# Four graph layers on one core: norm transfers first, gate and both attention layers in column groups, the sort in three pieces, the projection behind the dense loop

## The reference

```python
x = layernorm(x + gate(x, src, dst))
# g = tanh(x[dst] @ w_dst + x[src] @ w_src + b); z[dst] += x[src] * g * 0.5 * norm[dst] * norm[src]
x = layernorm(x + gat(gat(x)))
# per layer, two heads: h = x @ W; logits = leaky_relu(a_s.h[src] + a_d.h[dst], 0.2), self edges added
# a = softmax of the logits over the edges of one dst; out[dst] += h[src] * a
x = layernorm(x + cos(x, src, dst))
# softmax over each dst of beta * cosine(x[dst], x[src]); out[dst] += alpha * x[src]
x = layernorm(x + ((x + segsum(relu(x[src] + edge_attr @ Wl + bl), dst)) @ Wn + bn))
```

## Time and profile before

| what | us |
| --- | --- |
| median of 3 runs | 4987.31 (4984.94 to 4987.55) |
| the profiled execution's own time | 4982.04 |
| its span | 4980.2 |
| busy: PE / DVE / ACT / POOL | 1413.6 / 2485.9 / 960.6 / 3104.6 |
| setup and norms | 0 to 82.45 |
| node block | 82.45 to 1326.5 |
| gate block | 1326.5 to 1537.3 |
| attention 1 / attention 2 | to 2224.0 / to 2916.7 |
| cosine / message | to 3983.9 / to 4980.2 |

### The profile page before, as it was taken

The page is one execution under the profiler, slowest core; times in us unless marked ns, Lnnn a source line. Parts: engine busy times, 40 slices in busy tenths (PEclk is TensorE's granted clock), DMA queues, the critical chain, the costliest instruction groups (busy, mean ns, idle before and its releaser), DMA issues. The chain is left out here.

```text
span 4980.2 us, 34974 instructions
## 1 busy us (share of the span) xinstructions
PE 1413.6 (28%) x5413; PEld 1227.2 (25%) x5413; DVE 2485.9 (50%) x5048; ACT 960.6 (19%) x2420; POOL 3104.6 (62%) x2417
## 2 busy tenths in 40 slices
PE   2887047772031000763400000000000075053121
PEld 2887046762031000542200000000000054042111
DVE  4665036661387819763058853335664343252354
ACT  1554024441021000221100012221000044032010
POOL 6777777777405761017761037777648777787687
PEclk9555555555555555555555555555555576556555
DMA  3665135552011110223402345553001155243011
GB/s 79 183 187 164 21 87 137 138 141 49 3 40 36 22 21 2 80 80 90 113 19 59 104 112 144 144 144 102 15 11 18 19 157 138 66 113 91 16 18 17
DMA packets 285614, 395.98 MB, mean 80 GB/s; under 512 B 125970, under 2 KB 130829, under 8 KB 285562
## 3 DMA queue, kind: packets, MB, share of 16 engines
q1 hardware_dynamic: 170362, 322.94, 21.8%
q0 software_dynamic: 115200, 72.57, 8.9%
HBM read 183.71 MB, written 210.76 MB: 79 GB/s over the span
## 5 line engine op out<-in xcount | busy, mean ns | idle before, releaser
L754 PE MATMUL banks<-ident,cross_in 125*2 125x125 f32 (+3 forms) x26 | 10.5, 405 | 2210.7 <-DVE cross_in L777 1559.2
L210 POOL DMA_INDIRECT edge_rows<-x_rows,src_i x400 | 489.4, 1224 | 151.4 <-issue 151.4
L540 PE MATMUL banks<-node_w,x_t 65*125 65x200 f32 x1600 | 550.4, 535 | 0.0
L754 PEld LDWEIGHTS banks<-ident,cross_in 125*2 125x2 f32 (+3 forms) x26 | 3.0, 117 | 2215.3 <-DVE cross_in L777 1562.3
L540 PEld LDWEIGHTS banks<-node_w,x_t 65*125 65x125 f32 x1600 | 513.0, 328 | 4.7 <-issue 0.3
L210 POOL DMA_INDIRECT edge_rows<-h_rows,src_i x200 | 242.6, 1213 | 409.2 <-POOLq L1318 333.7
L210 POOL DMA_INDIRECT edge_rows<-x_rows,key_i x200 | 250.1, 1250 | 366.5 <-DMA norm_s<-sorted_pairs 296.7
L223 POOL DMA_INDIRECT x_rows<-r_x,src_scat_i x200 | 258.6, 1293 | 120.4 <-issue 60.6
L210 POOL DMA_INDIRECT edge_rows<-x_rows,dst_place_i x200 | 272.3, 1362 | 74.1 <-issue 74.1
L210 POOL DMA_INDIRECT edge_rows<-in_x_dram,src_i x200 | 254.6, 1273 | 78.1 <-issue 71.7
L223 POOL DMA_INDIRECT norm_rows<-edge_rows,scat_i x200 | 256.5, 1282 | 75.0 <-issue 75.0
(11 more groups left out here) (321 smaller groups left out, 4824.9 us busy)
## 6 DMA issues: line engine op xcount, KB each, us to landing
h_rows<-r_h SPq DMA_DIRECT2D x125, 462.0 KB
x_rows<-r_x SPq DMA_DIRECT2D x125, 241.5 KB
x_rows<-r_x SPq DMA_DIRECT2D x125, 224.0 KB
r_x<-x_rows SPq DMA_DIRECT2D x125, 224.0 KB
x_rows<-n_out SPq DMA_DIRECT2D x125, 224.0 KB
n_in<-in_x_dram SPq DMA_DIRECT2D x100, 224.0 KB
n_c<-x_rows SPq DMA_DIRECT2D x100, 224.0 KB
out_dram<-n_out SPq DMA_DIRECT2D x100, 224.0 KB
```

Source lines behind the costliest of these rows:

```text
L210: g.indirect_dma_start(out=to[:, j, :] if len(to.shape) == 3 else to[:, j:j + 1], out_offset=None, in_=table, in_offset=bass.IndirectOffse ...
L540: done = pe.matmul(product[h][:, n // 2, n % 2, :], x_t[u][:, at:at + P], node_w[:, :], start=True, stop=True)
L754: pe.transpose(bank[0][0:cols, 0:rows], frm, ident[0:rows, 0:rows]).then_inc(s_tout, 1)
```

## The change

PALL is 125, as P is, and where planes and rows "over all partitions" are named anew they are the same tiles. The constants, blocks and waits change as follows.

- **Node block**: POOL's transfers are put in the order norm scatters, norm gathers, x[src], x[dst]; the dots leave the node loop. The gate block is merged into it: behind the loop DVE sorts (piece one of three: 36 exchanges and 8 direct steps, and 30 and 54 exchanges in the pieces that follow; before, piece one had 91 and piece two 29), does the x[src] dots, and then the gate group by group of 32, 40, 40, 40, 32 and 16 columns, each behind the arrival of its x[dst] columns. A group's scans start from the last column of the group before. PE, ACT and SP have the projection between the node loop and the gate, in a form that starts the transposition of the next chunk before the product of this one.
- **First segments**: no carry is added to all columns any more. What comes from the partition before only changes the row at the end of the partition's first segment, and is put right at the block's end: one row per partition is fetched (`first_i`), corrected and scattered back.
- **Attention 1 and 2**: no maximum over the segment ahead of the exponents. A running maximum and a running sum are kept per head; the scans of the features are scaled at each column by the change of the maximum. After each group's scans, the node's own edge is merged, ACT makes the own rows (sixteen activations of 125x64 per chunk) and DVE adds them. POOL weighs nothing any more. In attention 2, PE adds the five terms of a chunk by matmuls with the identity and nothing is centred, as the weights are centred in the setup.
- **Scans**: a link stands behind every second scan, everywhere.
- **Cosine and message blocks**: the groups of columns are the new ones; the last has two chunks.

```diff
-GROUPS = (0, 10, 18, 22, 24, 25)
+PALL = 125
+GROUPS = (0, 4, 9, 14, 19, 23, 25)
+SCANS_BETWEEN = 2
...
 def sum_rows_dve(dve, rows, carry):
     for f in range(D):
         done = dve.tensor_tensor_scan(rows[:, :, f], cont[:, :], rows[:, :, f], 0.0, ALU.mult, ALU.add)
-    v.link(done)
+        if f % SCANS_BETWEEN == SCANS_BETWEEN - 1:
+            v.link(done)
...
-CUT = STEPS.index(("direct", SLOT_BITS - 1))
-PARTS = ((0, CUT), (CUT, len(STEPS)))
+CUTS = [0, STEPS.index(("direct", F_BITS + 1)), STEPS.index(("direct", F_BITS + 4)), len(STEPS)]
+PARTS = list(zip(CUTS, CUTS[1:]))
...
-gather(g, xs, x, src_i, s_gx, range(START[1], J))
-gather(g, xd, x, dst_i, s_gx)
-scatter(g, NORM, norm_place, scat_i, J, s_sn)
-g.wait_ge(s_sn, ALL)
-gather(g, norm_place_src, NORM, src_i, s_gn)
+scatter(g, NORM, norm_place_all, scat_i_all, J, s_norms)
+g.wait_ge(s_norms, 16 * J)
+gather(g, norm_place_src_all, NORM, src_i_all, s_norms)
+gather(g, xs_all, x, src_i_all, s_gx, range(START[1], J))
+gather_groups(g, xd_all, x, dst_i_all)
+for u in range(U):
+    g.wait_ge(s0.stored[u], ROWS_DONE * ((ECH + 1 - u) // 2))
+g.indirect_dma_start(out=fetched, out_offset=None, in_=X1,
+                     in_offset=bass.IndirectOffsetOnAxis(ap=first_i[:, :], axis=0)).then_inc(s_first, 16)
+g.wait_ge(s0.row, ECH + 1)
+g.indirect_dma_start(out=X1, out_offset=bass.IndirectOffsetOnAxis(ap=first_scat_i[:, :], axis=0), in_=first_x1, in_offset=None,
+                     bounds_check=last_row(g, ROWS), oob_is_err=False).then_inc(s_first, 16)
...
-nodes_dve(dve, gate_dots)
+nodes_dve(dve)
+sort_fill_dve(dve)
...
+sort_dve(dve, PARTS[0], held[0], held[1])
...
-sum_rows_dve(dve, xs, carry_rows[0])
+for n, (start, end) in enumerate(groups):
+    a, b = start * NC, end * NC
+    c = slice(a, b)
+    dve.wait_ge(s_got[n], got_done(n, 1))
+    dots(xd, 0, heads[0], (start, end))
+    dve.tensor_tensor(heads[0][:, c], heads[0][:, c], heads[1][:, c], ALU.add).then_inc(s0.tanh_in, 1)
+    dve.wait_ge(s0.tanh, n + 1)
+    v.link(dve.scalar_tensor_tensor(heads[0][:, c], heads[0][:, c], 0.5, norm_d[:, c], ALU.mult, ALU.mult))
+    v.link(dve.tensor_tensor(heads[0][:, c], heads[0][:, c], norm_place_src[:, c, 0], ALU.mult))
+    for i in range(start, end):
+        w = slice(i * NC, i * NC + NC)
+        v.link(dve.tensor_tensor(xs[:, w, :], xs[:, w, :], wide(heads[0][:, w]), ALU.mult))
+    for f in range(D):
+        done = dve.tensor_tensor_scan(xs[:, c, f], cont[:, c], xs[:, c, f], xs[:, a - 1, f:f + 1] if a else 0.0, ALU.mult, ALU.add)
+        if f % SCANS_BETWEEN == SCANS_BETWEEN - 1:
+            v.link(done)
+    for i in range(start, end):
+        step(i)
...
-dve.wait_ge(s_shared, 1)
-sums = (xa[:, :, 0:D], vb)
-for h in range(H):
-    sum_rows_dve(dve, sums[h], carry_rows[h])
+def running_softmax(dve, s, rows, at, n, sums, weigh):
+    a, b = (NC * c for c in groups[n])
+    c = slice(a, b)
+    for h in range(H):
+        done = dve.tensor_tensor(scales[:, 2 + h, c], rows[:, c, at + h], dens[h][:, c], ALU.add)
+    v.link(done)
+    for h in range(H):
+        done = dve.scalar_tensor_tensor(scales[:, 2 + h, c], scales[:, 2 + h, c], 0.2, scales[:, 2 + h, c], ALU.mult, ALU.max)
+    v.link(done)
+    for h in range(H):
+        done = dve.tensor_tensor_scan(peaks[:, h, a + 1:b + 1], pen_f[:, c], scales[:, 2 + h, c], peaks[:, h, a:a + 1], ALU.add, ALU.max)
+    v.link(done)
+    for h in range(H):
+        dve.tensor_tensor(scales[:, 2 + h, c], scales[:, 2 + h, c], peaks[:, h, a + 1:b + 1], ALU.subtract)
+        done = dve.tensor_tensor(scales[:, h, c], peaks[:, h, a:b], peaks[:, h, a + 1:b + 1], ALU.subtract)
+    v.link(done)
+    for h in range(H):
+        done = dve.scalar_tensor_tensor(scales[:, h, c], scales[:, h, c], 0.0, pen_f[:, c], ALU.min, ALU.add)
+    done.then_inc(s.args, 1)
+    dve.wait_ge(s.exps, 2 * n + 1)
+    for h in range(H):
+        done = dve.tensor_tensor_scan(masses[:, h, c], scales[:, h, c], scales[:, 2 + h, c], masses[:, h, a - 1:a] if a else 0.0, ALU.mult, ALU.add)
+    v.link(done)
+    for i in range(*groups[n]):
+        v.link(weigh(dve, slice(i * NC, i * NC + NC)))
+    for h in range(H):
+        for f in range(D):
+            done = dve.tensor_tensor_scan(sums[h][:, c, f], scales[:, h, c], sums[h][:, c, f], sums[h][:, a - 1, f:f + 1] if a else 0.0, ALU.mult, ALU.add)
+            if f % SCANS_BETWEEN == SCANS_BETWEEN - 1:
+                v.link(done)
...
+for n, (start, end) in enumerate(groups):
+    dve.wait_ge(s_got[n], got_done(n, 2))
+    running_softmax(dve, s1, xa, D + 1, n, sums, weigh)
+    merge_own(dve, s1, n, 1.0)
+    for i in range(start, end):
+        u, c, w = i % 2, slice(i * NC, i * NC + NC), slice((i - start) * NC, (i - start) * NC + NC)
+        parts = (n_sq[u], n_in[u])
+        for h in range(H):
+            done = dve.tensor_tensor(parts[h][:, :, :], sums[h][:, c, :], wide(mixes[:, h, w]), ALU.mult)
+        v.link(done)
+        dve.wait_ge(s1.own, i + 1)
+        for h in range(H):
+            done = dve.tensor_tensor(e_dup[u][:, :, h, :], e_dup[u][:, :, h, :], parts[h][:, :, :], ALU.add)
+        done.then_inc(s1.x, 1)
...
+def own_chunk(i):
+    u = i % 2
+    act.wait_ge(s1.loaded[u], ROWS_DONE * (i // 2 + 1))
+    if i >= 2:
+        act.wait_ge(s1.turned, i - 1)
+        act.wait_ge(s1.mixed[u], ROWS_DONE * (i // 2))
+    for c in range(NC):
+        at = i * NC + c
+        for h in range(H):
+            done = nc.scalar.activation(e_dup[u][:, c, h, :], r_x1[u][:, c, 0:D], ACT.Copy, scale=tops[h][:, at:at + 1])
+    done.then_inc(s1.own, 1)
...
-project_pe(pe)
...
-project_act(act)
...
-project_sp(sp)
+project_pe(pe)
+project_act(act)
+project_sp(sp)
...
+    terms = (n_in[u][:, :, :], n_c[u][:, :, :], r_x1[u][:, :, 0:D], e_dup[u][:, :, 0, :], e_dup[u][:, :, 1, :])
+    for k, term in enumerate(terms):
+        done = pe.matmul(cols3(bank[1 + i % 4][0:P, :]), ident[0:P, 0:P], term, start=k == 0, stop=k == len(terms) - 1)
+    done.then_inc(s2.y, 1)
```

1100 lines of the change are left out of this document (684 added, 416 removed).

## The result

The changed kernel takes 4604.09 us (median of 4 runs, 4600.04 to 4609.52) against 4987.43 (4984.94 to 4989.89) of the kernel before beside it: ratio 0.9232, interval 0.9216 to 0.9248. It is 383 us faster. The forecast was 4520, the range 4390 to 4670; the profiled execution has a span of 4598.2 us where the forecast had 4512.

A forecast was written before the change was run, and what follows sets the result against it. No engine was busy throughout; POOL's 760 transfers set the node block, waits held DVE elsewhere. Terms: node block and gate -145, attention -174 and -131, cosine +8, message -26, sum -468: span 4512, forecast 4520 us, range 4390 to 4670.

The forecast's parts named there:

- I charge nothing for DVE and POOL at the same time: Whole kernel: DVE and POOL working together slow neither, at 0 us, except where scans have no wait between them.
- 64 scans 13: Gate: the 64 scans of a 40-column group take DVE 13 us of about 50 us per group.
- the tail: Gate's end: carry by PE, one row fetched, corrected and scattered; estimated at 18.5 us.
- the terms added on PE, 5 x 0.885 = 4.4: Attention 2 mixing: PE's five terms take 4.4 us a chunk and, with ACT's 3.7 us of copies, pace it.
- The pair of 0.51: Attention blocks: two short scans with a linked wait behind the second take 0.51 us; bounds 0.3 and 0.545.
- The links let POOL in: Message block: links between scans end the 27.29 us gather stall, making the block 26 us shorter.
- the 165.3 us that were to go: Attention 2: DVE's 165.3 us wait for a transposition queued behind the projection goes when the projection moves.
- A: Scans beside gathers: links do not let POOL in, gathers stall for whole runs; 4560 to 4670, taken at 4610; chance 0.17.
- B: Linked scans beside gathers: each pair waits for one POOL transfer, 1.2 us per link; 4790 us; chance 0.05.
- C: Attention mixing: PE's clock rises, 7.1 falls towards 4.5 us a chunk, -65 per attention block; 4390 us; chance 0.11.
- D: Gate and attention scans: a fixed slot whatever the width, 0.545 us instead of 0.23; 5060 us; chance 0.04.
- E: Node block: projection ends at 1220, so the gate's normalising waits for PE and ACT; 4626 us; chance 0.02.

The follow-up runs named there:

- The two kernels on the ring: Attention 2: changed kernel without PE's two own-row terms, 4583.95 us; version with links in message block alone, h rows' load issued after ACT's copies, 4465.83 us.

## Why the prediction was right, and where it was off

**Direction, order and mechanism held.** POOL sets the node block's length and its end is followed by the last groups; the 760 transfers are the same; the sort moves into DVE's wait (73 us in the sum, 73 measured); the projection costs nothing where it is; the last groups of the cosine block cost what was said (+8, +6.4 measured). The time fell by 383 us where 467 were forecast. Of the signs named beforehand the node loop's end (900), attention 1 (524) and the longest transfer (1.74 us) came; the gate's end (1415.5, said 1380 to 1410) and attention 2 (606 from block to block, said 550 to 580) did not.

**What was off, 86 us in five terms.**

- Node block and gate, +23. Some 12 of it is POOL: its last x[dst] column ends at 1339.6 where about 1328 was forecast. "I charge nothing for DVE and POOL at the same time" was the wrong step. It isn't the linked scans that stretch the transfers: beside the second group's they take 1224 ns on the mean, and beside the normalising and the dots that follow 1341 (columns as in the earlier trace rows):

```profile
L223 POOL DMA_INDIRECT edge_rows<-in_x_dram,dst_i x11 | 13.5, 1224 | 3.4 <-issue 3.4
```

```profile
L223 POOL DMA_INDIRECT edge_rows<-in_x_dram,dst_i x27 | 36.2, 1341 | 10.5 <-issue 10.5
...
1167.06 1.73 POOL L223 DMA_INDIRECT edge_rows<-in_x_dram,dst_i  x1 [0.30 <-issue]
```

  In the old order the 200 norm gathers stand beside an idle DVE and take 1211 ns each; in the changed kernel they stand beside the node loop and take 1284. Another 5 us are the last two groups, which have nothing beside them: the step "64 scans 13" took the price of a scan from a constant start, and from memory, with the link's true price, 40 columns took 17.2 us, these two 16.1 and 14.2. The last 7 are the tail, 25.8 us where 18.5 was an estimate. In it DVE waits 9.5 us for the carry's transposition, which PE has queued behind the last chunk's rows:

```profile
1399.50 0.06 DVE L818 MEMSET crossed<- 64x1 f32 x1 [9.51 <-PE banks L789]
```

- Attention 1, +11: a pair of scans of 40 columns is 0.54 and not 0.51, 2 us in each of three groups; for 32 and 16 columns it is under 0.51. The rest is up to 2 us of mixing a group and 2 us in the last group and the tail.
- Attention 2, +44: "the terms added on PE, 5 x 0.885 = 4.4". The sum takes 7 us for the first chunk of a pair, and the load of own rows behind it was in no term; 6 of the 44 are in the scans and most of the others in the mixing. The two kernels on the ring give 20 us for two terms of five and 27 for the load.
- Message block, +9: the stall went, and the second 200 gathers end 22.8 us earlier, not 26. The 20 gathers beside linked scans of 200 columns take 1.36 us each, 3 us in all. The other 6 us are spread over the block's first and last 200 transfers, and why is open.
- Cosine block, -2.

**The hidden error.** The pair of 0.51 was nearly right by luck: it had the link at next to nothing and the scan too dear. An unlinked pair is 0.40, and the link is 0.14. So the sum was good for the kernel as it stands and blind for the question that matters: are the links worth it? They cost 96 us in both attention blocks and win 21 in the message block. "The links let POOL in" was right, and it pays in the message block and in the gate's first set. And the 165.3 us that were to go were no gain of their own. Two smaller readings were wrong and nothing hangs on them: attention 2 had 64 scans before, not 128 (384 long ones are those of all six sets, 256 of them replaced), and POOL's pauses come every 39 transfers in most stretches, not every 41.

**The rivals.** A (links don't let POOL in) fell: with them no gather is longer than 1.74 us. Its price was also too high: without links the first groups' scans hold POOL for 8 us in the gate and 16 in each attention block, and DVE then starts the gate's next groups 6 to 7 us later and waits 2 us more in attention 1. B (they alternate, 1.2 us a link) fell: 0.12 to 0.14 us a link, POOL or no POOL beside it (the gate of the kernel before has no gathers beside it, and the price is 0.12). The Trainium skill, "SBUF — State Buffer", section "SBUF: two separate sides", has the lock for a whole instruction: under sets of unlinked scans gathers do stand still for 8, 16 or 30 us, which is far more than one instruction, and under 40 columns from memory they don't, so the trace agrees with a lock and not with its length. C (cheaper mixing) fell: attention 1's clock is 0.55, and a group of five chunks takes 33.6 to 35.5 us to merge and mix where 33.5 was forecast. D (a fixed slot) fell: 16, 32 and 40 columns are 0.44, 0.50 and 0.54 a linked pair. E (the projection in the way) fell.

## What to carry to other kernels

A link between two instructions of one engine costs their overlap, not the idle time that the profile shows behind it: here 0.12 to 0.14 us, some four times the 0.03 of the gap, so put links only where another engine must get in and where the linked engine isn't the one waited for. When an engine's long wait is followed by a second wait for something that runs by itself, the first can be covered entirely, as the 165.3 us were: read what ends last. And in a ring of two buffers, release each buffer by its own last reader, not by the end of the stage.
